# Next-but-two quad of x requested by ScalarE on its own DMA queue, in a conditioned residual kernel

## The reference

```python
x = x + conv1d(x, L0_weight, padding=4, groups=4) + ctx[:, :, None] + fside_S_0[None, :, None]
for L in (L1, L2, L3):
    att = softmax(mlp(cond_128))                      # [128, 8]
    agg_w = einsum('bk,koi->boi', att, L.weight)      # one 64x64 matrix for each batch row
    x = x + einsum('boi,bih->boh', agg_w, x) + (att @ L.bias_k)[:, :, None]
return x
```

## Time and profile before

| | |
|---|---|
| median of 3 runs | 299.75 us (298.91 to 301.86) |
| profiled execution | 300.04 us |
| its span on the core | 298.2 us |
| TensorE (PE) busy | 279.2 us, 94% |
| ScalarE (ACT) busy | 188.0 us, 63% |
| VectorE (DVE) busy | 153.5 us, 51% |
| GpSimd (POOL) busy | 97.8 us, 33% |
| SyncE's queue (q1), share of the 16 DMA engines' time | 93.5% |
| moved by DMA | 104.55 MB, mean 351 GB/s |

### The profile page before, as it was taken

The page is one execution under the profiler, slowest core; times in us unless marked ns, Lnnn a source line. Parts: engine busy times, 40 slices in busy tenths (PEclk is TensorE's granted clock), DMA queues, the critical chain, the costliest instruction groups (busy, mean ns, idle before and its releaser), DMA issues.

```text
span 298.2 us, 6921 instructions
## 1 busy us (share of the span) xinstructions
PE 279.2 (94%) x1991; PEld 194.2 (65%) x1991; DVE 153.5 (51%) x198; ACT 188.0 (63%) x250; POOL 97.8 (33%) x269
## 2 busy tenths in 40 slices
PE   8898999999899998999999999999999999999982
PEld 7577766666666665666666766666667666666741
DVE  4683864554454445554445544455445545455333
ACT  4665566656567666666667676656667676666642
POOL 2510384441222341444452523411425223414100
PEclk9999999999999999999999999999999999999999
DMA  7869478999999999999999999999999999999887
GB/s 224 238 212 344 166 260 342 377 348 342 349 360 377 361 375 407 381 379 397 386 355 409 387 382 378 383 378 361 369 385 368 375 378 384 376 410 390 333 314 287
DMA packets 30627, 104.55 MB, mean 351 GB/s; under 512 B 3364, under 2 KB 5156, under 8 KB 22921
## 3 DMA queue, kind: packets, MB, share of 16 engines
q1 hardware_dynamic: 30546, 104.29, 93.5%
q10 hardware_dynamic: 72, 0.15, 0.2%
HBM read 36.26 MB, written 33.55 MB: 234 GB/s over the span
## 4 chain that ended last, share of the span: by engine, by line
PE 64%; DMA 24%; SPq 4%; ACT 2%; issue 2%; DVE 1%; ACTq 1%; POOL 0%; DVEq 0%; POOLq 0%
PE bank L406 43%; DMA y_sb<-conv_sb 22%; PE bank L450 15%; PE bank L535 2%; SPq L252 2%; DMA out_sb<-conv_sb 2%; PE bank L422 2%; ACT conv_sb L624 2%; SPq L276 1%; PE bank L506 1%; PE bank L473 1%; ACTq L637 1%; ACT L640 0%; POOL table L333 0%; PE bank L483 0%
## 5 line engine op out<-in xcount | busy, mean ns | idle before, releaser
L347 POOL COPY a<-table 64x64 f32 (+1 forms) x256 | 91.9, 359 | 170.2 <-PE bank L422 118.7
L624 ACT ACTIVATE conv_sb<-bank 128x512 f32<-128x512 f32 x128 | 73.7, 593 | 50.1 <-PE bank L406 49.5
L729 DVE TENSOR_TENSOR x_lo<-x_sb,x_hi 128x2064 fp32r<-128x2064 f32 x31 | 71.6, 2311 | 54.9 <-ACT x_hi L617 51.0
L406 PE MATMUL bank<-x_hi,toep_hi 128*128 128x512 f32 x256 | 84.5, 411 | 0.3 <-DVE x_lo L811 0.3
L746 DVE TENSOR_SCALAR out_sb<-bank,beta 128x512 f32<-128x512 f32 x62 | 46.6, 751 | 70.3 <-PE bank L450 69.6
L406 PE MATMUL bank<-x_hi,toep_lo 128*128 128x512 f32 x256 | 80.9, 398 | 0.0
L406 PE MATMUL bank<-x_lo,toep_hi 128*128 128x512 f32 x256 | 80.8, 397 | 0.0
L450 PE MATMUL bank<-y_sb,mixw 64*64 64x512 f32 (+1 forms) x520 | 62.6, 594 | 9.8 <-DMA y_sb<-conv_sb 8.1
L617 ACT ACTIVATE x_hi<-x_sb 128x2064 fp32r<-128x2064 f32 x31 | 59.7, 1927 | 10.2 <-DMA x_sb<-in_x 10.0
L631 ACT ACTIVATE out_sb<-bank,beta 128x512 f32<-128x512 f32 x62 | 42.6, 688 | 34.9 <-PE bank L450 33.6
L406 PEld LDWEIGHTS bank<-x_lo,toep_hi 128*128 128x128 f32 x256 | 48.3, 189 | 12.0
(11 more groups left out here) (74 smaller groups left out, 63.0 us busy)
## 6 DMA issues: line engine op xcount, KB each, us to landing
y_sb<-conv_sb SPq DMA_DIRECT2D x128, 256.0 KB, 6.2
x_sb<-in_x SPq DMA_DIRECT2D x31, 1032.0 KB, 8.3
out<-out_sb SPq DMA_DIRECT2D x29, 1024.0 KB, 8.1
out<-out_sb SPq DMA_DIRECT2D x4, 512.0 KB, 4.1
x_sb<-in_x SPq DMA_DIRECT2D x2, 516.0 KB, 10.2
out_sb<-conv_sb SPq DMA_DIRECT2D x8, 128.0 KB
x_sb<-in_toep SPq DMA_DIRECT2D x1, 640.0 KB, 7.4
out<-x_sb SPq DMA_DIRECT2D x1, 512.0 KB, 3.2
```

The costliest lines, as they stand in the source:

```text
L347: nc.gpsimd.tensor_copy(dst[rows, par, :, NH * e:NH * e + NH], table[n][C * e:C * e + C, here, h, :]).then_inc(comp_in, 1)
L406: last = mm(o, w[:, d, g, :], v[:, par, g, :, d:d + J], start=i + d == 0, stop=i + d == 3)
L624: nc.scalar.activation(conv_sb[:, par, g, :], conv_ps[g % banks][:, :], ACT.Copy).then_inc(conv_out, 1)
L729: nc.vector.tensor_tensor(x_lo[:, par].rearrange("p g s j -> p (g s j)"), x_sb[:, par].rearrange("p g s j -> p (g s j)"), x_hi[:, par].rea ...
```

## The change

`load` becomes a function of the issuing engine. SyncE still loads x1, x2, x3 and x4, and in its steps from 3 on it neither waits for x_hi and x_lo nor loads. ScalarE's step q, behind the copy of group 2, waits until x_hi and x_lo of quad q + 1 are written and then loads x of q + 3 into the half of quad q + 1, on ScalarE's own queue. It does so in steps 2 to 28, which is x5 to x31. The last two steps of ScalarE's loop are unrolled, since step 29 has nothing left to load.

```diff
+        def load(eng, q, par):
+            eng.dma_start(x_sb[:, par].rearrange("p g s j -> p (g s j)"),
+                          x_h[bass.ds(q * 128, 128), :]).then_inc(x_in[par], 16)
...
             def step(q, par):
-                sp.wait_ge(xhi_set, q + 1)
-                sp.wait_ge(xlo_set, q + 1)
-                load(q + 2, par)
+                if isinstance(q, int) and q < 3:
+                    sp.wait_ge(xhi_set, q + 1)
+                    sp.wait_ge(xlo_set, q + 1)
+                    load(sp, q + 2, par)
                 move(q, par, 0, par)
...
                 x_high(q + 1, it_next, 1 - par)
                 for g in range(G):
                     conv_copy(q, it, par, g)
+                    if g == 2 and (not isinstance(q, int) or q + 3 < NQ):
+                        act.wait_ge(xhi_set, q + 2)
+                        act.wait_ge(xlo_set, q + 2)
+                        load(nc.scalar, q + 3, 1 - par)
                 for p in range(PR):
                     finish(q - 1, it_prev, 1 - par, p)
...
-            with act.Fori(PEEL // 2, NQ // 2 - 1) as it:
+            with act.Fori(PEEL // 2, NQ // 2 - 2) as it:
                 step(2 * it, it, 0, it, it - 1)
                 step(2 * it + 1, it, 1, it + 1, it)
+            step(NQ - 4, NQ // 2 - 2, 0, NQ // 2 - 2, NQ // 2 - 3)
+            step(NQ - 3, NQ // 2 - 2, 1, NQ // 2 - 1, NQ // 2 - 2)
```

More of the change, by code:

```diff
@@ L234, in cond_resid_kernel @@
         block = ctx.enter_context(nc.Block())
+        def load(eng, q, par):
+            eng.dma_start(x_sb[:, par].rearrange("p g s j -> p (g s j)"),
+                          x_h[bass.ds(q * 128, 128), :]).then_inc(x_in[par], 16)
         @block.sync
         def _(sp):
-            def load(q, par):
-                sp.dma_start(x_sb[:, par].rearrange("p g s j -> p (g s j)"),
-                             x_h[bass.ds(q * 128, 128), :]).then_inc(x_in[par], 16)
             def store(q, par):
@@ L278, in _ @@
             sp.wait_ge(toep_lo_set, 1)
-            load(1, 1)
+            load(sp, 1, 1)
             sp.wait_ge(xhi_set, 1)
             sp.wait_ge(xlo_set, 1)
-            load(2, 0)
+            load(sp, 2, 0)
             for g in range(G):
```

## The result

The changed kernel takes 316.02 us at the median of 4 runs (314.68 to 317.02), against 300.29 for the old one beside it (298.91 to 301.86). The ratio is 1.052, with a 95% interval of 1.045 to 1.059: it is slower by 5%, where 298.0 was forecast. A second set of runs gave 314.43 and 1.047 (1.038 to 1.056). The profiled execution took 315.73 us, its span 313.8. Some executions of a kernel come out slow, most of them at a lower granted clock (one of `f6` took 391.5 us at 0.66); medians and ranges here are of all runs, ratios and their intervals of the others.

The account below looks back on a forecast made before the run. Nearly full DMA engines were taken as the bound, with the excess showing as TensorE's waits for regroupings. From the profiled 300.04, -0.6 (order), -1.1 (rate) and -0.3 (issue) gave 298.0 us, own range 295.5 to 301, whole range 291.5 to 306.5.

Parts of the forecast that it names:

- what bounds the kernel: Loop steps: full DMA engines are just about the bound, 8.31 us a step against TensorE's 7.95; the excess becomes TensorE's waits.
- the 292.4 worked out for 393 GB/s: Rival that the DMA rate rises to 393 GB/s throughout: 300.0 - 7.6 = 292.4 us, chance 0.31.
- the costs on ScalarE: x issue between copies of groups 2 and 3: 0.58 us, fitting idle time with 0.18 to spare, cost 0.
- SyncE's issue: SyncE's queue without x loads: 0.7 us of issue may leave the loop; 0.3 us gain put in the sum.
- the rate: DMA transfer rate in the loop: a small rise from 375 to 377 GB/s, 27 x 0.04 = 1.1 us gained.
- all three terms of the sum: Order -0.6, rate -1.1 and a little of the issue -0.3 us, taken from the profiled 300.04.
- The lower bound: Worst DMA rate considered, 353 GB/s as from 65.6 to 83.4: 8.93 us a step, a loss of 16.7 us.
- The order: x served between and beside regroupings 2 and 3: net -2.0 to +0.8 us, with -0.6 in the sum.
- x pushing the last regrouping back: Rival: x, issued 1.2 us ahead of the last regrouping, lengthens the loop by 0.7, 14 times: 310 us, chance 0.12.
- Its mark, a share under 0.97: Sign of x pushing the last regrouping back: DMA share falls under 0.97 while the landings grow.

Follow-up runs that it names:

- f6: Old kernel with the loop's stores on ScalarE's queue, x left with the regroupings, a second set of runs: 292.66 us, ratio 0.976.
- f2: Changed kernel with x from x5 on copied from an on-chip table instead of read from HBM: 291.6 us.
- f1: Old kernel with x from x5 on copied from an on-chip table instead of read from HBM: 290.6 us.
- e1: Old kernel with x loaded on ScalarE's own queue, asked for at the old time: 323.6 to 330.1 us.
- e2: Old kernel with x of q+3 issued early, between regroupings 2 and 3, on SyncE's one queue: 329.2 to 354.0 us.
- e8: Changed kernel with ScalarE also issuing the last regrouping, x of q+3 right behind it on the same queue: 325.1 us, ratio 1.086.
- e10: Old kernel with stores on ScalarE's queue and x of q+3 on SyncE's queue between regroupings 2 and 3: 322.9 to 333.4 us.
- e11: Old kernel with both stores and x on ScalarE's queue, x asked for at the old time: 339.1 us, ratio 1.130.
- e7: Old kernel with the loop's stores on ScalarE's queue, x and regroupings on SyncE's in the old order: 291.53 us, ratio 0.971.
- e6: Changed kernel loading only half of each x tile from x2 on: 290.9 us, ratio 0.968.
- e5: Old kernel loading only half of each x tile from x2 on: 292.4 us, ratio 0.971.
- e9: Changed kernel with each x load cut into four transfers, one for each group, in rows of 2064 bytes: 348.8 us, ratio 1.155.

## Why the prediction was wrong

**Right: what bounds the kernel.** Bytes over rate, with the excess showing as waits for the last regrouping. The halved loads and the copies from on-chip memory bring 290.6 to 292.7, close to the 292.4 worked out for 393 GB/s, and there TensorE binds.

**Right: the costs on ScalarE.** Where 0.58 was put down (0.49 and 0.09), the issue takes 0.35 and the register work 0.09. The copy of group 3 begins at 156.08, 5.87 into the step from 150.21, where 5.9 was the mark. Its waits for x are gone. And as I wrote, this buys nothing.

**Right, with no use: SyncE's issue.** The lag between copy and issue fell from 0.8 us to 0.1, but the landing grew by 1.4 to 1.9 in the steps shown. I had written that the gain counts only if the landing doesn't grow.

**The step that failed: the rate.** "I take a small rise, to 377." It fell to 356. The rate's term was a gain of 0.04 us a step, 8.31 to 8.27; a step took 8.82. The 28 steps grew by 14.7 us, where all three terms of the sum together had taken 2.0 off. Add the 1.4 ahead of quad 2 and take off the 0.4 won back, and 14.7 + 2.0 + 1.4 - 0.4 are the 17.7 by which 298.0 missed the profiled 315.73. The lower bound was near the truth, 353 GB/s and 16.7 us lost. (It set 8.93, bytes over rate, against a measured 8.31 that is 8.41 by the same sum at 375; on one footing it is 27 x 0.52 = 14.0.) But neither a rival nor the range was given to it. Everything I called slower was a wait in the loop while the engines ran idle elsewhere. The choice of 377 rested on the sum of bytes, as if a byte had one price. But the rows showed between 353 and 393 GB/s at an almost full share, and I had written that "something makes a transfer slower at times". That was the place to ask what, and to price a fall to 353 like a rise to 393.

**The rule I weighed there.** The Trainium skill (DMA: Bandwidth & Descriptors, Issuing engines are not separate DMA queues) says that several issuing engines only save issue time. By it the rate's term was 0. The runs don't agree: which transfer goes to the second queue moves the time from 291.5 (stores, 399 GB/s) over 300.3 (none, 380) to 316.0 and more (x, 360), and not through issue time.

**The order.** My net of -2.0 to +0.8 is neither confirmed nor refuted: with reads it can't be told from the rate, and with copies (f2 is 1.05 us over f1, within their spread) TensorE sets the pace and would hide it.

**The rival that came nearest** was x pushing the last regrouping back (310, chance 0.12). Its sign and its place are right: landings are 1.4 to 1.9 longer in the steps shown. x doesn't take its share at once, as I wrote: its rows begin some 3 us after the request at 111.02, and then have the engines nearly to themselves. Its mark, a share under 0.97, isn't met in the changed kernel but is in e1, e2, e8, e10 and e11. Its reason, the place of x in the order, isn't enough: with x copied, in the same place, regroupings land after 4.3 us at the median.

**What stays open.** Why a read of HBM on a queue of its own, asked for this early, makes the rows of other transfers longer, regroupings within on-chip memory among them. One reading was that the old order lets each DMA engine get to x at a time of its own, while an empty queue starts x on all of them together. The rows speak for it only in part. At the median load from 100 to 250 us, the 128 rows begin within 4.2 us in the changed kernel (the first 16 within 0.5), and within 6.0 and 6.5 (1.1 and 1.2) in the old one and in e7. But in e1 and e2 they are spread as in the old kernel, 5.8 and 6.4 us, and in f2 they are closest of all, 2.3, at no cost. So beginning together costs only where HBM is read, if it is the cause at all, and it isn't the cause of e1's and e2's losses. Why engines go idle in those, and in e8, e10 and e11, is argued and not shown; e8, e10 and e11 were not repeated with copies.

## What to carry to other kernels

When the DMA share is full, read the GB/s beside it, stretch by stretch: if the same bytes take different times, the rate is a variable, and a change of order or queue is first of all a change of rate, to be bounded on both sides and given its chance on both. Ask also whose time has grown: here it was mostly that of transfers that nobody had touched. With reads from HBM, writes to HBM and on-chip copies at the limit together, it was the stores that could leave for the second queue (a gain of 2.4 to 2.9%), not the reads (a loss of 5%). And to take a wait off an engine that isn't on the path, here 9.6 us of ScalarE's, is worth nothing, but what is done for it can cost.

## What the runs showed of the hardware

- From 100 to 250 us, 3080 KB a step went at 360 GB/s (x read on a second queue), 380 (all on one), 399 (stores on the second) and 397 (x copied on chip), with the engines at 0.97 to 1.02 of their time. Within a step of the changed kernel the rate went from 430 to 280 GB/s at shares of 0.95 to 1.06.
- A row of 2048 bytes within on-chip memory took 84.0 ns at the mean in f2, without reads of HBM on the second queue, and 93.4 in the changed kernel with them (99.9 against 88.3 with half the reads, e6 and e5), but 84.2 and 86.8 with the reads on that queue at the old time (e11 and e1). A row of 8256 bytes took 312 ns from on-chip memory (f2) and 359 to 424 from HBM.
- Issues of loads on ScalarE took 0.34 to 0.37 us in the changed kernel, one at a time, and 0.65 to 1.03 from the second on when four of 258 KB followed each other in the step shown of e9. In e8, right behind the issue of a regrouping, they took 0.56 to 1.19 from 108 to 140 us.
- In e2, behind a landing of 9.4 us, TensorE's clock was at its lower level (0.50) and a mix took 3.69 us instead of 1.95. In the changed kernel, which waits at most 2.1 us at a time, the clock averaged 0.996.
